# The mixer's loop over eight groups, written out in constants

## The reference

```
proj = x_norm @ in_proj_w.T            # gate 8192, hBC 8192 + 2*8*128, dt 128
hBC  = silu(conv1d(hBC, 4 taps) + b)   # hidden hs, B and C per group
for each chunk of 128 tokens (8 chunks), for each of 128 heads (64 wide):
    Y_diag = (C B^T * exp(segsum(dt*A))) @ (hs*dt)
    Y_off  = exp(A_cum) * C @ state           # state carried over chunks
    state  = exp(A_last) * state + B^T (decay * hs*dt)
y = (Y_diag + Y_off + hs*D) * silu(gate)
out = groupnorm(y, 8 groups) * norm_w @ out_proj_w.T
```

## Time and profile before

| | us |
|---|---|
| median of 3 runs | 3077.02 |
| the profiled execution's own time | 3087.84 |
| its span, first to last instruction | 3086.0 |
| PE busy | 2793.9 |
| DVE busy | 2099.8 |
| ACT busy | 1018.0 |
| POOL busy | 736.9 |

### The profile page before, as it was taken

How to read it: one execution, slowest core, us unless ns; L and a number is a source line. 1 busy time by engine, 2 the same in 40 slices (tenths; PEclk the granted TensorE clock), 3 DMA queues, 4 the chain that set the end, 5 groups by cost and what they waited for, 6 DMA issues and landing times. The chain is left out here.

```text
span 3086.0 us, 48209 instructions
## 1 busy us (share of the span) xinstructions
PE 2793.9 (91%) x15936; PEld 1831.3 (59%) x15936; DVE 2099.8 (68%) x3247; ACT 1018.0 (33%) x2081; POOL 736.9 (24%) x576
## 2 busy tenths in 40 slices
PE   3799999989999998989999999999699979999889
PEld 2465666666665655665666566666487444444478
DVE  5586777668777677767767787786555646666364
ACT  1233233233332233233233233333211326666321
POOL 1232232232323322221332322323222001111031
PEclk7899999999999999999999999999899989999989
DMA  4101121120111111021111111201201311111000
GB/s 162 22 16 39 28 72 29 38 72 15 45 49 44 41 33 65 17 57 44 37 46 27 65 26 48 71 15 23 80 0 67 130 59 32 36 41 36 1 7 21
DMA packets 117075, 135.25 MB, mean 44 GB/s; under 512 B 28064, under 2 KB 88560, under 8 KB 114160
## 3 DMA queue, kind: packets, MB, share of 16 engines
q1 hardware_dynamic: 111392, 130.37, 14.9%
q10 hardware_dynamic: 5456, 2.00, 0.3%
HBM read 113.96 MB, written 18.38 MB: 43 GB/s over the span
## 5 line engine op out<-in xcount | busy, mean ns | idle before, releaser
L452 PE MATMUL bank<-xnT,wh 128*128 128x512 f32 x1280 | 578.7, 603 | 51.6 <-issue 26.2
L546 PE MATMUL bank<-xnT,wg 128*128 128x128 f32 x4096 | 480.5, 276 | 0.0
L546 PEld LDWEIGHTS bank<-xnT,wg 128*128 128x128 f32 x4096 | 467.9, 192 | 3.3 <-issue 3.3
L589 PE MATMUL bank<-wo,yt 128*128 128x512 f32 x1024 | 459.2, 602 | 6.4 <-DVE yt L841 6.2
L736 DVE SCALAR_TENSOR_TENSOR cacc<-raw,cwh,cacc 128x512 f32<-128x512 f32 x480 | 438.2, 913 | 17.0
L452 PEld LDWEIGHTS bank<-xnT,wh 128*128 128x128 f32 x1280 | 237.9, 192 | 326.4 <-issue 290.4
L589 PEld LDWEIGHTS bank<-wo,yt 128*128 128x128 f32 x1024 | 196.3, 193 | 249.1 <-issue 249.1
L939 POOL TENSOR_TENSOR rr<-rr,nhalf 128x1 f32<-128x1 f32 x64 | 35.2, 550 | 988.6 <-DVE rr L874 988.6
L733 DVE TENSOR_SCALAR cacc<-raw,cwh 128x512 f32<-128x512 f32 x160 | 142.4, 890 | 143.0 <-ACT raw L721 142.9
L643 ACT ACTIVATE cth<-cacc 128x512 f32<-128x512 f32 x160 | 101.6, 635 | 400.9 <-DVE cacc L736 400.9
L649 ACT COPY xs<-bank 128x512 f32<-128x512 f32 x128 | 74.5, 582 | 460.9 <-PE bank L478 460.9
(11 more groups left out here) (242 smaller groups left out, 4415.1 us busy)
## 6 DMA issues: line engine op xcount, KB each, us to landing
EC<-ecum_scratch SPq DMA_DIRECT2D x112, 256.0 KB
wh<-w_hs_dram SPq DMA_DIRECT2D x80, 256.0 KB, 10.7
wg<-w_gate_dram SPq DMA_DIRECT2D x8, 2048.0 KB, 8.4
wo<-w_out_dram SPq DMA_DIRECT2D x8, 2048.0 KB, 9.2
qk_scratch<-at_part SPq DMA_DIRECT2D x48, 256.0 KB
at_qT<-qk_scratch SPq DMA_DIRECT2D x32, 192.0 KB, 2.6
at_kT<-qk_scratch SPq DMA_DIRECT2D x32, 192.0 KB, 2.6
wgu<-w_gu_dram SPq DMA_DIRECT2D x1, 3584.0 KB, 11.4
```

Source lines behind the costliest of these rows:

```text
L452: mm = nc.tensor.matmul(BA[bank][:, :], wh[:, j, k, :], xnT[:, k, h * HALF:(h + 1) * HALF], start=(k == 0), stop=(k == KC - 1))
L546: mm = nc.tensor.matmul(BA[b][:, i * P:(i + 1) * P], wg[:, k, j * P:(j + 1) * P], xnT[:, k, ttok], start=(k == 0), stop=(k == KC - 1))
L589: mm = nc.tensor.matmul(BA[b][:, :], yt[:, j * P:(j + 1) * P], wo[:, j, :], start=(j == 0), stop=(j == JT - 1))
```

## The change

`groups` becomes a Python loop over all eight groups, so that the body is put down eight times on PE, DVE, ACT and POOL with g as an integer. SP's loop over g = 0 to 6 is also written out. The flag `last`, which was true only in the copy outside the loop, is now computed from g. The order of the instructions on each engine stays, and so do the buffers, the tiles and the DMAs; register arithmetic for waits and addresses and the jumps go, and waits that g = 0 doesn't need (a value of zero or less) are left out.

```diff
         def groups(eng, body):
-            with eng.Fori(0, G - 1) as g:
+            for g in range(G):
                 body(g)
-            body(G - 1)
...
             def body(g):
                 for z in range(NT):
-                    slot(eng, g, z, tiles_of(g, z), bank, isinstance(g, int) and z == NT - 1)
-                if not isinstance(g, int):
+                    slot(eng, g, z, tiles_of(g, z), bank, g == G - 1 and z == NT - 1)
+                if g < G - 1:
                     assert bank.now == 1
             groups(eng, body)
...
-                with sp.Fori(0, G - 1) as g:
+                for g in range(G - 1):
 
                     for z in range(4):
                         next_rows(g, z)
```

## The result

The changed kernel takes 3026.41 us (median of 4 runs, 3024.24 to 3033.24), the kernel before, run beside it, 3076.27 us (3075.28 to 3077.7). The ratio is 0.985, with an interval of 0.9836 to 0.9864: faster by 49.9 us. The forecast was 3027 us from 50.3 us. The sum is right; of its three terms the heads came out smaller and the loads larger, and these two errors largely cancel. A second set of runs on another chip gave 3031.04 against 3072.99 us (0.9866, 0.9851 to 0.9881).

A forecast was written before the change was run, and what follows sets the result against it. The prediction took TensorE as the bound, busy 2793.9 of 3086.0 us, with time to win only where it stands still or runs at its lower clock. Terms 38.4 + 5.9 + 6.0 = 50.3 us gave 3027 us, range 3008 to 3044.

The forecast's parts named there:

- Part 1: Mixer group heads (slots z = 0): without six taken jumps, groups 1 to 6 become like group 7, saving 38.4 us.
- The lower bound of 30 us: Group heads: the saving if each new `EC` wait is as long as 3 us instead of 1.57.
- Part 2: Plain mixer slots z = 1, 2, 5 and 6: constants replace register operations, 0.21 us each over 28 slots, 5.9 us.
- Part 3: Mixer slots z = 3 to 5: SP orders `EC` sooner, 15 waits in five groups shrink 0.4 us each, 6.0 us.
- for it: Slots z = 3 to 5: short waits keep PE's clock up, returning more than the wait; upper end 40.1 us.
- rival A: Slots z = 3 to 5: most `EC` waits fall away as PE keeps its clock, winning 25 us; 3008 us, chance 0.13.
- my own test: Slots z = 3 to 5, five slow groups: the forecast is wrong if these stretches leave 98 to 102 us.
- rival B: Loads collide more: `EC` waits grow 0.5 us in 15 slots and take 3 us at heads; 3049 us, chance 0.15.
- Part 4: Other engines' jumps, attention, FFN and the longer straight code's instruction fetching: cost 0.
- rival C: Mixer: straight code can't be fetched fast enough, so PE stalls inside groups; slower, 3139 us, chance 0.03.
- D: Group heads: the stall is not the jump's and stays; 3071 us if the constants alone pay, chance 0.03.
- The step from the profile to the median: Whole kernel: the profiled execution's 10.8 us over the median carried over whole, giving 3077.0 - 50.3 = 3026.7 us.

The follow-up runs named there:

- regs_straight: Against the kernel before: passes written out without jumps, the group's number still in a register that counts up; 3042.54 us, ratio 0.9892.
- hinted: Against the kernel before: loops and jumps kept, with a prefetch hint for the jump on PE, DVE, ACT and POOL; 3044.72 us, ratio 0.9911.
- pe_only: Against the kernel before: only PE's loop written out in constants, the other engines keep theirs; 3050.87 us, ratio 0.9916.
- sp_only: Against the kernel before: only SP's loop written out in constants, the other engines keep theirs; 3062.64 us, ratio 0.9967.
- before_again: The kernel before, unchanged, run and profiled a second time; 3070.15 us, ratio 1.0001.
- after_again: The changed kernel, with no further edit, run and profiled a second time; 3031.04 us, ratio 0.9866 to the kernel before.
- not_pe: Against the kernel before: loops of DVE, ACT, POOL and SP written out in constants, PE keeps its loop; 3060.13 us, ratio 0.9949.
- weigh_late: Against the changed kernel: POOL weighs `wo` only after DVE's `xch` product; 3020.17 us, ratio 0.9835 to the kernel before.
- ec_first: Against the changed kernel: `RW` and `EC` loads of slot z = 1 ordered ahead of the 2 MB of `wo`; 3038.48 us, ratio 0.9901 to the kernel before.
- wh_late: Against the changed kernel: SP waits until `EC` has landed before ordering the `wh` loads; 3010.66 us, ratio 0.9791 to the kernel before.

## Why the prediction was right, and where it was not

**The sum.** Forecast 3026.7, measured 3026.41. That exactness is luck: by terms, heads 38.4, constants 5.9, loads 6.0; measured in the first pair of profiles 30.7, some 6.2 (28 x 0.22) and 21.5, in the second 31.7, some 6.2 and 10.9. (The z = 5 slots of five groups are in both of the last two terms, so they overlap by about 1 us.) Each is the difference of two single profiles. The first pair's terms belong to the mixer's 57.7 us, not to the 49.9 us of the medians: the profiled execution of the kernel before was 11.6 us above its median, that of the changed kernel 1.5 us below.

**Part 1, the heads: right in mechanism, 7 to 8 us too large.** That the six taken jumps cause the stall and the low clock is shown from both sides: regs_straight and hinted. Group 7's slot was the right model for four heads of six, whose sum of 143.8 us is four times 35.95. The mis-sized part is "as in group 7" for all six: group 2 costs 3.6 us more by a collision, group 3 4.2 us more by an `EC` wait of 2.95 us and its clock. The trace of before did show the first: in all six loop heads `xch` took 4.3 to 5.3 us, because POOL's weighing was ahead of a late DVE. I counted the 1.24 us that PE waited for `sg`, but read it as DVE's late start and not as two engines that hold each other. With DVE on time, the weighing starts between 0.4 us before `xch` and 1.6 us after it, and who is first varies from run to run. The same weighing meets a later product of DVE in most heads as well (L840, 4.9 to 5.4 us in six of the seven), and PE does not wait for that one. The lower bound of 30 us, for `EC` waits of 3 us, did hold the result.

**Part 2, the constants: right in size, wrong in place.** 0.22 us per plain slot. The reason I gave for nothing as the lower end, that matmuls cover PE's sequencer, is in fact true: pe_only wins nothing there. It is the constants of DVE, ACT and POOL, taken together.

**Part 3, the loads: right in sign and in the wait, too small in all.** SP orders `EC` sooner, as forecast (3.56 us after the slot's start instead of 3.95, so 0.4), and no other engine's change matters (sp_only). The size is 10 to 21 us instead of 6.0. The mean of the five stretches over the five profiles in which SP has the group in a register (before, before_again, regs_straight, hinted, pe_only) is 502.5 us, over the six with SP in constants and these loads as they were (after, after_again, sp_only, not_pe, weigh_late, ec_first) 486.2: 16.3 us. The 15 waits for `EC` in them sum to 31.8 us in the mean of the first five (29.3 to 35.2) and to 23.0 in that of the six (21.6 to 24.5). That is 8.8 us, or 0.59 for each wait, where I took 0.4. The other half is clock: PE's busy time for the same matmuls falls by 8.5 us, from 468.3 to 459.8. I named this "for it", and rival A had a price for it, but I left it out of the sum. In the first pair alone PE's granted clock goes from 0.97 in all five stretches to 0.98 in three and 1.00 in two, and its busy time from 470.8 to 460.4 us. By my own test the stretches should have stayed between 98 and 102 us; they average 97.3, so rival A's mechanism was partly at work, in the stretches, while at one head (group 3) the longer wait of rival B was. The sum hides both.

**Part 4, what costs nothing: right.** Fewer blocks of instructions were loaded and PE has no "issue" gap inside a group, so rival C is out; the stall at the heads is gone, so D is out. ACT does show 30 gaps for "issue" ahead of L719, 66.0 us in all, where it had 5 with 8.7 us. Its waits at this line sum to 161.5 us, though, and were 171.1 before: they are most likely the same waits, put down to other causes.

**The step from the profile to the median** (the 10.8 us carried whole) was not as safe as I wrote it. The excess of that one profile lay in the five stretches, with their `EC` waits (35.2 us against 29.3 in before_again) and the clock: the same place as the third term. A term read from it is part noise.

## What to carry to other kernels

Where a loop's last pass already stands outside it, one trace holds both forms: take the price of the jump from the two heads, and the price of registers from the two plain slots. Before giving the difference to every pass, look at what varies between the passes (a load that lands early or late, two engines that are only just apart), because a freed engine walks into it. And read the passes that run well: two groups of seven showed what the stretches cost without `EC` waits, and a wait on SP that holds bulk loads back until the urgent one has landed gave that pace to all.

## What the runs showed of the hardware

- A taken jump back over the mixer's long body takes PE 3.3 to 5.7 us (24 jumps, in before, before_again, sp_only and not_pe), the one that falls through 0.083; with a prefetch hint at the start of the pass 0.44 to 0.49 us in five of six, and 4.23 in one.
- Next to a POOL tensor_tensor of 128x4096 in fp32 (7.02 us) that started first, a DVE tensor_tensor of 128x1024 takes 7.7 to 8.1 us instead of 1.23, and a tensor_scalar of 128x512 3.45 instead of 0.55. Where DVE was first, it kept its 1.23 us, and the POOL operation took 8.08 us when it started 0.02 us later. Three scalar_tensor_tensor of 128x512 took 5.36 us instead of 2.33 beside two POOL products of 128x1024.
- `wo` (2 MB) lands 7.7 to 9.4 us after its issue at the heads of the changed kernel. With the `EC` pair ordered 6.6 us ahead of it (ec_first) it takes 7.5 and 7.8 us at the heads of groups 2 and 6, and 11.3 to 13.8 at the other five.
- The `EC` pair (two loads of 256 KB) lands sooner in groups 2 and 6 than in the others, with the same loads around it: in wh_late SP gets past its waits for them 7.5 to 7.6 us after the second one's issue in groups 2 and 6, and 9.1 to 10.1 in the other five. The groups differ only in the addresses; that this is the cause was not tested.
